# Scales of routed expert weights from each partition's largest magnitude

## The reference

```python
x = x + attention(layernorm(x))              # x: 2 x 1024 x 512, float32
h = layernorm(x)                             # 2048 tokens of 512
scores = softmax(h @ gate_w)                 # 8 experts
topk_w, topk_idx = top_k(scores, 2)
g = silu(einsum('td,edh->teh', h, w_gate)) * einsum('td,edh->teh', h, w_up)   # 352 wide
routed = einsum('teh,ehd,te->td', g, w_down, comb)
shared = silu(h @ sw_gate) * (h @ sw_up) @ sw_down                            # 704 wide
out = x + routed + shared
```

## Time and profile before

| | |
|---|---|
| median of 3 runs | 720.23 us (717.61 to 724.28) |
| the profiled execution | 722.54 us, span 720.7 us, mean granted PE clock 0.977 |
| PE busy | 652.9 us (91%) |
| DVE busy | 441.8 us (61%) |
| ACT busy | 235.7 us (33%) |
| POOL busy | 215.5 us (30%) |

### The profile page before, as it was taken

One profiled execution on the slowest core, in us unless ns is written; L12 is line 12 of the kernel. 1 busy time (PEld: TensorE's weight loads), 2 busy tenths in 40 slices (PEclk: granted clock), 3 DMA queues, 4 the chain that ended last, 5 costly groups with the idle time before them and its releaser, 6 DMA issues.

```text
span 720.7 us, 11499 instructions
## 1 busy us (share of the span) xinstructions
PE 652.9 (91%) x3677; PEld 423.1 (59%) x3678; DVE 441.8 (61%) x808; ACT 235.7 (33%) x353; POOL 215.5 (30%) x234
## 2 busy tenths in 40 slices
PE   2979879789999689799999899999999999999992
PEld 2757657568668366356665565665556565656551
DVE  6878887987997864477787878633333333333331
ACT  4343432142342312346565665421111111111110
POOL 6100101201101113444343234124444444444331
PEclk9999999999999999899999999999999999999997
DMA  6840003420260468897574524258877777977762
GB/s 219 286 130 16 15 16 87 138 67 30 76 160 30 117 166 210 238 248 189 131 198 101 112 33 69 47 111 137 130 133 131 131 131 131 125 138 131 126 93 42
DMA packets 111235, 86.87 MB, mean 121 GB/s; under 512 B 79280, under 2 KB 86448, under 8 KB 111200
## 3 DMA queue, kind: packets, MB, share of 16 engines
q1 hardware_dynamic: 88848, 43.94, 25.7%
q0 software_dynamic: 12272, 27.34, 22.3%
q10 hardware_dynamic: 10080, 15.14, 7.0%
HBM read 44.45 MB, written 23.33 MB: 94 GB/s over the span
## 4 chain that ended last, share of the span: by engine, by line
PE 65%; DVE 17%; DMA 6%; issue 5%; ACT 2%; SPq 2%; ACTq 1%; POOL 1%; DVEq 0%; POOLq 0%
PE ps_y L504 17%; PE ps_g L504 15%; PE ps_u L504 15%; PE ring L378 12%; PE turn_h L524 3%; DMA shared<-in_L_attn_w_out_dram 2%; DVE run_kv L1205 2%; DMA routed<-in_L_ffn_w_down_dram 1%; DVE routed L1347 1%; ACTq L362 1%; DVE run_kv L1197 1%; DVE run_k L1193 1%; SPq L771 1%; DVE xn_hl L1282 1%; DVE num L1244 1%
## 5 line engine op out<-in xcount | busy, mean ns | idle before, releaser
L1287 DVE TENSOR_TENSOR hidT<-turn_h,hidT 128x384 f16<-128x384 f32 x71 | 39.5, 556 | 112.3 <-ACT hidT L1036 103.8
L911 POOL DMA_INDIRECT out_dram<-y_job,job_tok x39 | 61.8, 1585 | 106.6 <-DVE y_job L1638 85.8
L378 PE MATMUL ring<-xnT_h,wq_h 128*128 128x512 f32 x192 | 80.9, 421 | 11.2 <-DVE run_kv L1197 5.0
L1032 ACT ACTIVATE silu<-ps_g,job_silu 128x352 f32<-128x352 f32 x39 | 21.6, 553 | 190.9 <-PE ps_g L504 135.8
L504 PE MATMUL ps_y<-routed,hidT 128*128 x351 | 82.1, 379 | 1.4 <-DVE hidT L1287 1.3
L836 POOL TENSOR_SCALAR var_eps<-mean_var 128x1 f32<-128x1 f32 x32 | 11.8, 369 | 227.7 <-DVE mean_var L1268 125.8
L378 PE MATMUL ring<-xnT_h,wq_l 128*128 128x512 f32 x192 | 78.2, 407 | 0.0
L378 PE MATMUL ring<-xnT_l,wq_h 128*128 128x512 f32 x192 | 77.9, 406 | 0.0
L504 PE MATMUL ps_g<-routed,x_in 128*128 x468 | 76.4, 313 | 1.3 <-issue 1.2
L504 PE MATMUL ps_y<-shared,hidT 128*128 128x512 f16 x288 | 69.3, 387 | 7.6 <-DVE hidT L1287 7.5
L504 PE MATMUL ps_u<-routed,x_in 128*128 x468 | 76.2, 313 | 0.0
(11 more groups left out here) (222 smaller groups left out, 1063.0 us busy)
## 6 DMA issues: line engine op xcount, KB each, us to landing
routed<-in_L_ffn_w_gate_dram ACTq DMA_DIRECT2D x7, 704.0 KB, 4.9
routed<-in_L_ffn_w_up_dram ACTq DMA_DIRECT2D x7, 704.0 KB, 8.9
x_res<-in_L_attn_x_dram SPq DMA_DIRECT2D x18, 256.0 KB, 3.2
out_dram<-x SPq DMA_DIRECT2D x16, 256.0 KB, 3.3
xn_scratch<-xn_hl SPq DMA_DIRECT2D x16, 256.0 KB, 2.4
out_dram<-y_job POOLq DMA_DIRECT2D x16, 256.0 KB, 4.2
x_in<-in_L_attn_x_dram SPq DMA_DIRECT2D x14, 256.0 KB, 2.8
routed<-in_L_ffn_w_down_dram ACTq DMA_DIRECT2D x7, 512.0 KB, 10.9
```

The source lines that it names most:

```text
L378: ins = pe.matmul(ps, a, b, start=(i == 0), stop=(i == len(steps) - 1))
L911: pool.indirect_dma_start(out[:, :], bass.IndirectOffsetOnAxis(job_tok[:, r:r + 1], 0), y_job[:, b, :], None, compute_op=ALU.add).then_inc ...
L1032: act.activation(silu[:, :], ps_g[:, 0:F], ACT.Silu, scale=by).then_inc(s["silu_s"], 1)
L1287: dve.tensor_tensor(hidT[:, 1], turn_h[:, 0:FC, :], hidT[:, 0], ALU.subtract).then_inc(s["hidT_s"], 1)
```

## The change

The scales of the routed pieces no longer come from squares. DVE itself reduces each raw piece to one largest magnitude per partition (largest), squares the three numbers of an expert (top_sq), PE sums these over the partitions with one matmul of 3 columns (bound), and set_scales takes four times that sum as the bound. The squares of ACT, the folds of POOL, and the column norms of PE go for the 24 routed pieces; the 6 pieces of the shared expert keep them. The wait for an expert's weights moves from ACT's square to DVE's reduction.

The core of the diff (two buffers and three semaphores are added besides):

```diff
-        norm_unit = lambda u: SHARED_PIECES + u - NORM_UNIT if NORM_UNIT <= u < NORM_UNIT + 3 * E else None
+        norm_unit = lambda u: u - NORM_UNIT if NORM_UNIT <= u < NORM_UNIT + 3 * E else None
+        bound_unit = lambda e: NORM_UNIT + 3 * e + 4
...
+        bound_of = lambda e: ps_norm[:, 3 * e:3 * (e + 1)]
...  PE, in unit u, ahead of the down product
-                if norm_unit(u - 1) is not None:
-                    column_norms(norm_unit(u - 1))
+                for e in range(E):
+                    if u == bound_unit(e):
+                        pe.wait_ge(s["top_sq_s"], e + 1)
+                        pe.matmul(bound_of(e), ones_h[:, :], top_sq[:, e, :], start=True, stop=True)\
+                            .then_inc(s["bound_mm"], 1)
...  POOL
-                for u in (2 * t, 2 * t + 1):
-                    if norm_unit(u) is not None:
-                        fold(norm_unit(u))
...  ACT
-                if norm_unit(u) is not None:
-                    square(norm_unit(u))
...  (in upper)
+                if x < E and kind == 0:
+                    act.wait_ge(s[f"w{x}"], 16 * 4)
...  DVE
+            def largest(m):
+                e, kind, h, w, done = pieces[SHARED_PIECES + m]
+                if kind == 0:
+                    dve.wait_ge(s[f"w{e}"], 16 * 4)
+                elif e == 0 and kind == 2:
+                    dve.wait_ge(s["over_0"], 2)
+                dve.tensor_reduce(top_w[:, e, kind:kind + 1], w, AX_X, ALU.max,
+                                  apply_absolute_value=True).then_inc(s["top_w_s"], 1)
+                if kind == 2:
+                    dve.wait_ge(s["top_w_s"], m + 1)
+                    dve.tensor_tensor(top_sq[:, e, :], top_w[:, e, :], top_w[:, e, :], ALU.mult).then_inc(s["top_sq_s"], 1)
...  (in set_scales)
-                dve.wait_ge(s["max_s"], SHARED_PIECES + 3 * (n - 1))
+                if x == E:
+                    dve.wait_ge(s["max_s"], SHARED_PIECES)
+                else:
+                    dve.wait_ge(s["bound_mm"], x + 1)
...
-                set_link(dve.tensor_scalar(big, big, 2.0 ** -120, None, ALU.max))
+                    set_link(dve.tensor_scalar(big, big, 2.0 ** -120, None, ALU.max))
+                else:
+                    set_link(dve.tensor_scalar(big, bound_of(x), 4.0, 2.0 ** -120, ALU.mult, ALU.max))
...  DVE, in unit u, behind hidden(u + 1) and one_hots
                 if norm_unit(u - 1) is not None:
-                    column_max(norm_unit(u - 1))
+                    largest(norm_unit(u - 1))
```

More of the change, by code:

```diff
@@ L87, in preln_decay_attention_moe @@
         part_max = sb("part_max", [P, 3, 2])
+        top_w = sb("top_w", [P, E, 3])
+        top_sq = sb("top_sq", [P, E, 3], BF16)
         col_max = sb("col_max", [P, SETS, 3])
@@ L248, in preln_decay_attention_moe @@
             gw_h_s gw_l_s gate_mm logit_s x2_out0 x2_out1 xn2_out0 xn2_out1 pad_out cst_a cst_b shared_in
-            over_0 w0 w1 w2 w3 w4 w5 w6 w7 square_s fold_s norm_mm max_s set_s upper_s split_s
+            over_0 top_w_s top_sq_s bound_mm w0 w1 w2 w3 w4 w5 w6 w7 square_s fold_s norm_mm max_s set_s upper_s split_s
             d_set d_route rt_exp rt_exp_in picked_s hot_s route_mm tables_s xin0 xin1 gin0
@@ L296, in norms_of @@
             n = pieces[m][3].shape[1] // 4
-            return ps_gate[:, P:P + n] if m < SHARED_PIECES else ps_norm[:, 0:n]
+            return ps_gate[:, P:P + n]
+        bound_of = lambda e: ps_norm[:, 3 * e:3 * (e + 1)]
         FREE_PARTS = 2 * KC
@@ L912, in scatter @@
                                         y_job[:, b, :], None, compute_op=ALU.add).then_inc(s[f"yo{b}"], 16)
-            def fold(m):
-                half = pieces[m][3].shape[1] // 2
-                pool.wait_ge(s["square_s"], m + 1)
-                pool.tensor_tensor(squares[:, 0:half], squares[:, 0:half], squares[:, half:2 * half], ALU.add)\
-                    .then_inc(s["fold_s"], 1)
             const(pool.memset(zeros[:, :], 0.0))
@@ L937, in _ @@
                 gather(r)
-                if r == 0:
-                    for u in range(2 * (NT - AHEAD + 1), HALVES * NT):
-                        if norm_unit(u) is not None:
-                            fold(norm_unit(u))
                 if r < AHEAD - 1:
@@ L993, in square @@
                     act.wait_ge(s["over_0"], 1)
-                elif x < E and kind == 0:
-                    act.wait_ge(s[f"w{x}"], 16 * 4)
-                elif x == 0 and kind == 2:
-                    act.wait_ge(s["over_0"], 2)
                 if m:
```

## The result

The changed kernel takes **732.15 us** (median of 4 runs, 730.26 to 734.24) against 719.02 for the kernel before in the same job (4 runs, 717.61 to 724.28): ratio 1.0164, 95% interval 1.0132 to 1.0195. It is slower by 1.6%. The profiled execution took 730.83 us, with a span of 729.1 and a mean granted clock of 0.967, where before had 722.54, 720.7 and 0.977.

The account below looks back on a forecast made before the run. PE, busy 91% of the span, was taken to bound the kernel. Waits and savings summed to +5.8 us, clock falls added +4.7; +10.5 on the 720.2 us median gave 731 us, range 722 to 737.

Parts of the forecast that it names:

- the late bound: Experts 4 to 7: set_scales waits for PE's matmul behind the up product; 18.9 us of waits in units 19, 22, 25, 28.
- waits in units 10 and 16: DVE has one_hots, set_scales and a split there, 6.6 us, so PE waits 1.9 us in each.
- wait in unit 5, for ACT's issue: ACT issues two experts' loads for 9.5 us, making rest_hidT of unit 5 late; PE waits 3.4 us.
- clock, second stage: PE falls to half clock behind the four waits of 4 to 6 us: +4.7 us, bounds 0 and +8.
- first stage: From unit 5's gate product to unit 9's: four units of 5.85 us plus waits, forecast at 27.15 us.
- second stage, with the clock: From unit 9's gate product to the first routed product, clock falls included: forecast at 165.2 us.
- Neither saves time by itself: ACT loses 24 squares, POOL 24 folds; only what they held up, in units 4 and 19, counts.
- the short waits: PE waits for DVE's extras in units 10, 13 and 16 and for split pieces in unit 20: together 5.5 us.
- That the clock would hold: Rival: the waits come without clock falls, +5.8 us, 726 us, within 1%; chance 0.20.
- DVE would become the bound: Rival: slower reductions or more clock falls cost units 10, 13 and 16 more, 733 to 737 us; chance 0.12.
- Rival 3: Short waits and unit 5's wait vanish, leaving the late matmul's waits: +1.6 us, 722 us, not slower; chance 0.08.
- The late bound is a wait: Denied by a rival: matmul for experts 4 to 7 lands a unit earlier, no waits or falls, 708 us; chance 0.04.

Follow-up runs that it names:

- experiment 3: The changed kernel, with PE multiplying data nobody reads ahead of the down products of units 19, 22, 25 and 28: 729.17 us, ratio 1.0114.
- the repeat: The changed kernel run once more, unchanged, in a later job: 731.76 us, ratio 1.0153.
- Experiments 1 and 2: First: changed kernel, set_scales of experts 4 to 7 reading the preceding expert's sum, 714.28 us; second: kernel before with only the late matmul wait added, 741.71 us.
- experiment 7: The changed kernel with ACT's old wait for expert 0's weights put back in unit 3, ahead of the softmax's exp: 733.06 us, ratio 1.0158.
- experiment 4: The changed kernel with each reduction reading only the first 352 of its piece's 1408 or 1536 columns: 731.59 us, ratio 1.0159.

## Why the prediction was right

The forecast, 731 and slower by over 1%, held: the median is 732.15, the ratio 1.0164 where 731 over 720.2 is 1.0150. Step by step:

| step | forecast | measured |
|---|---|---|
| the late bound, from the small matmul's start to the down product's | 4.3, 4.45, 5.9, 4.45, less 0.2: 18.9 | 4.03, 4.16, 5.58, 4.15: 17.9 |
| idle time of PE in these | 4 to 6 | 3.73, 3.86, 5.41, 3.98: 17.0 |
| DVE idle in front of each | 2 to 3.5 | 1.96, 3.49, 3.49, 3.39 |
| waits in units 10 and 16 | 1.9 each | 1.48, 1.47 |
| wait in unit 20 | 1.4 | hidden behind the fall; 1.39 with the clock held (experiment 3) |
| wait in unit 5, for ACT's issue | 3.4 | 2.99 |
| issue of two experts' loads | 9.5 | 9.94 |
| a reduction of 1408; of 1536 | 1.62; 1.76 | 1.61; 1.75 |
| set_scales; split of 1408 | 1.75; 1.60 | 1.58; 1.60 |
| clock, second stage | +4.7 | 5.05; 7.0 against the repeat (experiment 3) |
| clock, first stage | 0 | 2.7; 0 in the repeat |
| first stage | 27.15 | 30.39, and 27.53 with the clock held |
| second stage, with the clock | 165.2 | 164.3; 166.2 in the repeat |
| both stages against before | +10.5 | +12.9; +11.9 in the repeat |

*The late bound.* Right in place, count and size. The 1.0 between 18.9 and 17.9 lies in two pieces that come four times: the hand-over took 0.24 (389.65 to 389.89) where I took 0.35, and set_scales 1.58 (389.89 to 391.47) where I took 1.75. Experiments 1 and 2 show the wait from both sides.

*The clock.* Right in kind in the second stage and close in size: 4.7 for 5.05, or for 7.0 against the repeat. The window view has 0.50 to 0.55 behind each late wait, and the stage at full clock is 159.26 for 164.31. The reading "3 us at half speed lose 1.5" was low: a fall cost between 1.3 and 2.9, 1.7 and 2.1 on the mean of the two executions. The Trainium skill (TensorE: Matmul & The Clock Gate, HAM oscillation) has the mechanism, and this trace agrees with it: the clock was given up again at each of the four waits. In experiment 7 one of the four held. **The term that was missing** is in the first stage. I priced unit 5's wait at 3.4 and no fall behind it, though by my own reading of the earlier trace rows (a toss-up at 2 us, a fall at 3.03 close upon another wait) 3.4 should have cost one. It did: the down product took 4.02 for 2.12 and the next gate product 2.74 for 1.95, together 2.7. That is more than the difference between 10.5 and 12.9; the rest of the first stage came out 0.4 above the forecast and the second stage 0.9 below it. In the repeat there was no fall there, and the four others cost 1.9 more. In five executions with the same order of work up to there, waits of 2.79 to 3.12 brought a fall three times and none twice, so a chance of a half and some 1.4 us would have been the fair price.

*ACT and POOL.* "Neither saves time by itself" fits: 32 and 42 us less for them, and PE's stages are longer. What they held up in unit 4 was put down to ACT's wait for the weights. Experiment 7 doesn't bear that out: with the wait back, PE waits 2.18 there and the time is the same.

*DVE.* Its load in the stretch was forecast at 164 and is 145.19. Reductions are as priced (39.7 for 40). The rest, some 17 us, is work that had been stretched in the kernel before and isn't any more: 24 splits take 41.4 instead of 45.9, and the small operations of set_scales have come down to what they take alone. In the rows of the kernel before every operation that took over 0.1 us more than its shortest has a fold of POOL beside it: eleven splits and steps of set_scales, 12.3 us over their shortest, and three steps of routing, 3.8 us. The prediction used the stretched figure as DVE's base load. For the time this mattered little, since DVE was not the bound (experiment 4). For units 10 and 16 the terms add up to 6.4 and not to the 6.6 that is written; 6.4 less the 4.5 gives the 1.9.

*The sum.* That 731 came so near is luck in part. The late bound (1.0) and the short waits (some 0.9) were priced too high, the clock too low. The mechanism, four waits of PE and a half clock behind them, doesn't rest on that.

*The rivals.* That the clock would hold (726) is excluded by the windows and by experiment 3, that DVE would become the bound by experiment 4. Rival 3 wanted the short waits and the one in unit 5 gone: they stayed, at 1.48, 1.47 and 2.99. The late bound is a wait, and DVE's earlier dates did not help it: in experiment 4 DVE got there earlier still, and PE's waits were the same.

What these runs leave open is how the 2.8 us by which the first stage became shorter divide among squares, folds and norm matmuls, as told under experiment 7.

## What to carry to other kernels

When a value goes from engine A to engine B and back to A, look up in both queues what stands ahead of the hand-over: here PE's matmul of 0.17 us stood behind a product of 1.95, DVE waited with everything queued behind it, and four such places cost 18 us with the clock. Read PE's wait, not the busy share of the engine that makes it wait: 27 us less work on DVE was worth nearly nothing, and the same work in another order was worth 4% of the program. Count a fall of the clock, 1.3 to 2.9 us in these runs, behind a PE wait of 3.7 to 5.5 us: it came in 23 of 24 such waits.

## What the runs showed of the hardware

*DVE operations beside a POOL fold.* In the kernel before, one operation on 3 numbers took 1.50 us. DVE there:

```profile
323.22 0.17 DVE L1330 TENSOR_SCALAR unscale<-unscale 128x3 int32<-128x3 int32 x1
323.42 1.50 DVE L1331 TENSOR_SCALAR scale<-unscale 128x3 int32<-128x3 int32 x1
```

and POOL:

```profile
323.38 1.51 POOL L918 TENSOR_TENSOR squares<-squares 128x704 bf16<-128x704 bf16 x1 [3.99 <-ACT squares L1000]
```

The operation started 0.04 behind the fold and ended 0.03 behind it. In the changed kernel, without folds, the same operation (L1341) takes 0.17 every time. The Trainium skill (SBUF — State Buffer, Who interferes with whom) says that the two engines share a pair of ports that one of them holds for a whole instruction, and that the order of issue decides who is blocked; these rows agree. It also says that a reduction never takes part in this. The reductions of the kernel before read PSUM, and four of them that started inside a fold (329.86, 342.29, 380.75, 422.29) took 0.52 as elsewhere, which fits. For the long ones from SBUF no run here can show it: with them the folds were gone.

*The clock behind waits of 2 to 3 us is not fixed by the wait.* In unit 5, with the same order of work before it, PE went on at half speed after 2.99, 3.12 and 2.88 (down products of 4.02, 4.02 and 3.58), and at full speed (2.12) after 2.88 and 2.79: the same 2.88 has both. Behind the 24 waits of 3.7 to 5.5 (the four late ones, in six executions) it fell 23 times; once, in experiment 7, it held after 3.86. The trace of the kernel before had more rows on this than the prediction used: of seven waits of 2.05 to 2.52 in its attention, four had three us at 1.00 behind them (17.04, 94.85, 100.62, 162.09) and three a fall within three us (51.78, 143.56, 255.33), and behind one of 5.35 (246.69) the clock was 0.50 for three us.

*The price of issuing loads.* The four loads of one expert, issued by ACT, held it for 2.9 us, and the next expert's right behind them for 7.0 (291.54 to 298.49); issued 2.9 us later they took 4.3. What of the queue makes the later ones longer is not shown here.
